# Channel attention, tile 0: where the rests, the row statistics and the second batch's projection stand

## The reference

```python
def _L0_xattn_ref(x, init, Wq, bq, Wk, bk, Wv, bv):   # init is ctx_4096
    q = jnp.einsum('dc,bct->btd', Wq, init) + bq
    k = jnp.einsum('dc,bct->bdt', Wk, init) + bk[None, :, None]
    R = jnp.einsum('btd,bds->bts', q, k)
    attention = jax.nn.softmax(R, axis=-1)
    v = jnp.einsum('oc,bct->bto', Wv, x) + bv
    return jnp.einsum('bts,bsc->bct', attention, v)
...
x = x + jnp.tanh(g_xattn[0]) * _L0_xattn_ref(_layernorm(x, axis=-1), ctx_4096, ...)
```

## Time and profile before

| what | value |
|---|---|
| median of 3 runs | 847.76 us (847.03 to 848.78) |
| the profiled execution's own time | 845.51 us |
| its span | 843.7 us |
| busy: PE, PEld | 774.3 us (92%), 613.4 us (73%) |
| busy: DVE, ACT, POOL | 662.9 us (79%), 352.3 us (42%), 380.9 us (45%) |
| HBM traffic | 44 GB/s over the span |

### The profile page before, as it was taken

One profiled execution on the slowest core, in us unless ns is written; L12 is line 12 of the kernel. 1 busy time (PEld: TensorE's weight loads), 2 busy tenths in 40 slices (PEclk: granted clock), 3 DMA queues, 4 the chain that ended last, 5 costly groups with the idle time before them and its releaser, 6 DMA issues.

```text
span 843.7 us, 12571 instructions
## 1 busy us (share of the span) xinstructions
PE 774.3 (92%) x4276; PEld 613.4 (73%) x4276; DVE 662.9 (79%) x1230; ACT 352.3 (42%) x1064; POOL 380.9 (45%) x324
## 2 busy tenths in 40 slices
PE   2898998888989999999999999999999999969975
PEld 1565565786867788888878888877888787757754
DVE  5788888888978877778788777787877778798972
ACT  2777776221334333333333333434333243237541
POOL 2787787415364433333253332434423333386541
PEclk9999999897999999999999999999999999989995
DMA  8310030101021111011020100102101020200101
GB/s 256 107 51 25 25 106 0 39 0 51 1 76 50 38 38 51 26 38 39 26 63 26 51 26 26 48 29 63 38 26 38 26 88 24 55 4 1 38 25 38
DMA packets 37460, 37.43 MB, mean 44 GB/s; under 512 B 2912, under 2 KB 27232, under 8 KB 37408
## 3 DMA queue, kind: packets, MB, share of 16 engines
q1 hardware_dynamic: 35184, 32.81, 13.3%
q10 hardware_dynamic: 2224, 3.94, 1.5%
HBM read 34.64 MB, written 2.10 MB: 44 GB/s over the span
## 4 chain that ended last, share of the span: by engine, by line
PE 63%; DVE 6%; POOL 4%; issue 3%; ACT 2%; POOLq 0%; DVEq 0%; ACTq 0%
PE QB L1478 6%; PE QB L1480 6%; PE SB L1598 6%; PE QB L1479 6%; PE ROW L1479 6%; PE ROW L1478 6%; PE ROW L1480 6%; PE KV L1478 4%; PE PB L1571 3%; PE KV L1479 3%; PE KV L1480 3%; DVE rope_b L1244 2%; PE KV L1662 2%; PE TB L1541 2%; POOL dense L976 1%
## 5 line engine op out<-in xcount | busy, mean ns | idle before, releaser
L976 POOL TENSOR_TENSOR dense<-rope_a,rope_b 128x512 f32<-128x512 f32 x62 | 79.4, 1280 | 167.5 <-DVE rope_b L1244 167.3
L1110 ACT ACTIVATE ot_hi<-PB 128x512 fp32r<-128x512 f32 x64 | 38.3, 599 | 198.4 <-PE PB L1571 198.2
L1101 ACT ACTIVATE e_sb<-masked,nmax 128x64 f32<-128x64 f32 x256 | 86.1, 337 | 58.1 <-DVE nmax L1273 57.7
L1478 PE MATMUL QB<-xT_hi,wq_lo 128*128 128x512 f32 x256 | 107.0, 418 | 0.0
L1479 PE MATMUL ROW<-wo_lo,ot_hi 128*128 128x512 f32 x256 | 101.7, 397 | 0.0
L1480 PE MATMUL QB<-xT_hi,wq_hi 128*128 128x512 f32 x256 | 101.7, 397 | 0.0
L1479 PE MATMUL QB<-xT_lo,wq_hi 128*128 128x512 f32 x256 | 101.5, 396 | 0.0
L1478 PE MATMUL ROW<-wo_hi,ot_lo 128*128 128x512 f32 x256 | 101.3, 396 | 0.0
L1480 PE MATMUL ROW<-wo_hi,ot_hi 128*128 128x512 f32 x256 | 101.0, 395 | 0.0
L1241 DVE TENSOR_TENSOR rope_a<-QB,rope 128x512 f32<-128x512 f32 x62 | 42.8, 691 | 72.7 <-PE QB L1480 72.5
L1282 DVE TENSOR_TENSOR p_sb<-e_sb,rz 128x256 f32<-128x256 f32 x64 | 86.8, 1356 | 2.2
(11 more groups left out here) (200 smaller groups left out, 1902.2 us busy)
## 6 DMA issues: line engine op xcount, KB each, us to landing
raw<-in_wq SPq DMA_DIRECT2D x32, 256.0 KB, 2.7
raw<-in_wo SPq DMA_DIRECT2D x32, 256.0 KB, 2.6
ctx_two<-in_ctx SPq DMA_DIRECT2D x16, 256.0 KB, 3.8
x_sb<-in_x SPq DMA_DIRECT2D x8, 256.0 KB, 7.1
ctx_raw<-in_ctxT ACTq DMA_DIRECT2D x1, 2048.0 KB, 12.9
raw<-in_wv SPq DMA_DIRECT2D x8, 256.0 KB, 2.7
raw<-in_wk SPq DMA_DIRECT2D x8, 256.0 KB, 2.9
out<-x_sb SPq DMA_DIRECT2D x8, 256.0 KB, 2.0
```

What stands on the lines that cost most here:

```text
L976: nc.gpsimd.tensor_tensor(dst, a, b, ALU.add).then_inc(s_rot, 1)
L1101: nc.scalar.activation(e_sb[:, r, :], masked[:, r, :], ACT.Exp, bias=nmax[:, r:r + 1], accum_out=zsum[:, r:r + 1]).then_inc(s_exp, 1)
L1478: nc.tensor.matmul(out, lhs[1], rhs[0], start=first, stop=False)
```

## The change

VectorE makes the two rests of tile 0's first batch ahead of any row statistics; of these it makes only those of tiles 0 and 1 in front of tile 0, and those of tiles 2 to 7 one by one in the units 2 to 7 of tile 0, behind the unit's maximum. The variance step and the power step are each made twice, for tiles 0 and 1 and for tiles 2 to 7; the second power step stands on GpSimd behind tile 0. Tile 0's second batch is projected behind the scores of unit 0 and rounded in unit 1. The eighth of ctx_raw that belongs to tile 0 is rounded in unit 7. GpSimd's tile 0 stands outside its loop. Three small loads are issued by SyncE behind the contexts.

```diff
@@ block.sync
                 load_ctx(t)
+            sp.dma_start(c["bias0"][:, :], d["bias0"].partition_broadcast(P)).then_inc(c["s_small"], 16)
+            sp.dma_start(c["assign_i"][:, :], d["assign"].partition_broadcast(CLUSTERS)).then_inc(c["s_small"], 16)
+            sp.dma_start(c["cluster_id"][:, :], d["cluster_ids"]).then_inc(c["s_small"], 16)
             load_ahead(sp, d, c)
@@ block.scalar, tile
-                    if u == PROJECT_B + 1:
+                    if u == (PROJECT_B + 1 if behind else 1):
                         qk_round(t, 2)
                         qk_round(t, 3)
...
-                    if u == OUTPUT:
+                    if u == (OUTPUT if behind else 7):
                         act.wait_ge(s_raw, 16)
                         nc.scalar.activation(ctx_hi[:, t, :], ctx_raw[:, t, :], ACT.Copy).then_inc(s_thi, 1)
@@ block.scalar
-            act.dma_start(c["bias0"][:, :], d["bias0"].partition_broadcast(P)).then_inc(c["s_small"], 16)
-            act.dma_start(c["assign_i"][:, :], d["assign"].partition_broadcast(CLUSTERS)).then_inc(c["s_small"], 16)
-            act.dma_start(c["cluster_id"][:, :], d["cluster_ids"]).then_inc(c["s_small"], 16)
@@ block.vector, tile
-                    if u == PROJECT_B + 1:
+                    if u == (PROJECT_B + 1 if behind else 1):
                         qk_rest(t, 2)
                         qk_rest(t, 3)
+                    if u >= 2 and not behind:
+                        dve.wait_ge(s_x[u], 16)
+                        row_sums(nc, dve, c, u, s_sum, s_mv, u)
                     if u == OUTPUT:
                         inverse(t, u)
-                        if not behind:
-                            dve.wait_ge(s_rstd, 1)
+                        if behind < 2:
+                            dve.wait_ge(s_rstd, behind + 1)
                         normalize(t)
...
+                if not behind:
+                    dve.wait_ge(s_mv, TILES)
+                    variance_eps(nc, c, s_var, 2, TILES)
@@ block.vector
-            for t in range(TILES):
+            qk_rest(0, 0)
+            qk_rest(0, 1)
+            for t in range(2):
                 dve.wait_ge(s_x[t], 16)
                 row_sums(nc, dve, c, t, s_sum, s_mv, t)
-            dve.wait_ge(s_mv, TILES)
-            variance_eps(nc, c, s_var)
-            qk_rest(0, 0)
-            qk_rest(0, 1)
+            dve.wait_ge(s_mv, 2)
+            variance_eps(nc, c, s_var, 0, 2)
@@ block.gpsimd
-            def tile(t, ahead):
+            def tile(t, ahead, first=False):
...
-                    if u == OUTPUT:
+                    if u == (7 if first else OUTPUT):
                         eighth_rest(t)
...
-            inverse_deviation(nc, pool, c, s_var, s_rstd)
-            with pool.Fori(0, TILES - 1) as t:
+            inverse_deviation(nc, pool, c, s_var, s_rstd, 0, 2)
+            tile(0, True, True)
+            inverse_deviation(nc, pool, c, s_var, s_rstd, 2, TILES, 2)
+            with pool.Fori(1, TILES - 1) as t:
                 tile(t, True)
@@ block.tensor, tile
-                    if u == PROJECT_B:
+                    if u == (PROJECT_B if behind else 0):
                         project(t, 2)
                         project(t, 3)
```

## The result

The kernel after takes 850.71 us (median of 14 runs, 848.36 to 853.05); the kernel before, run beside it, 846.00 us (14 runs, 844.37 to 848.78). The ratio estimated from these runs is 1.0045, with a 95% interval of 1.0034 to 1.0056, which is 3.8 us; the two medians themselves lie 4.71 us apart. Forecast were 3.4 us more, a ratio of 1.0040. The profiled execution took 850.24 us around a span of 848.2 us, 4.73 us above that of before.

The account below looks back on a forecast made before the run. VectorE, full from tile 0's sixth maximum to tile 1's first, was taken as the bound. Start -2.15 plus tile 0 longer +5.6 made +3.4 after rounding: 847.76 became 851.2 us; eight in ten, 848.9 to 853.4.

Parts of the forecast that it names:

- Start, -2.15: First score matmul: with the rests first, TensorE starts when w_v lands, at 15.65 instead of 17.80, a gain of 2.15 us.
- Early projection and moved stall: Tile 0, units 0 to 2: second maximum 19.5, VectorE's 1.4 us idle moved to unit 1, fourth maximum 2.2 us late.
- Path to the sixth maximum, 6.31 - 1.14: Tile 0, fourth to sixth maximum: 6.31 us loses two roundings of 1.14, so 5.17; sixth maximum at 29.7, 1.07 late.
- rival (5): TensorE's clock falls in the sparser tile 0; projections and scores take 1.2 us more, 852.4 us; chance 0.05.
- From the sixth maximum, +2.5: Sixth maximum to tile 1's first: three more pairs (2.4) and a variance step (0.1) lengthen VectorE's 4.88 us by 2.5.
- The cover of the pairs of units 3 and 4: VectorE's statistics there (1.6 us) lie under the path to the sixth maximum; without cover, nothing up to 1.6 more.
- GpSimd, taken as 0: Between tiles 0 and 1: eighth_rest and second power step, together 2.6 us, taken as 0, with 2.6 as bound.
- a sign of being wrong: The forecast is wrong if the shift at tile 1 is not the shift at the end of the stage.
- Variance step, taken as 0.1: End of tile 0: the new variance step shifts its follower by 0.1 us; bounds 0.1 and 1.1 beside a GpSimd product.
- Rival (2), statistics in the waits: The statistics vanish in VectorE's waits, tile 0 keeps its length, only the earlier start counts: 845.6 us; chance 0.06.
- Rival (6): Statistics stretched by GpSimd through the shared port, some 0.6 us for each of six, 3.9 us more: 855.1; chance 0.03.

Follow-up runs that it names:

- wv_early: The kernel after with the two transfers of w_v issued ahead of x; 846.37 us, ratio to before 0.9992.
- fill_more: The kernel after with 8, 8 and 16 unread matmuls added behind the scores of units 2, 3 and 4 of tile 0; 848.05 us, ratio to before 1.0018.
- eighth_back: The kernel after with tile 0's eighth of ctx_raw rounded in unit 3 and its rest made there by GpSimd, as before; 850.09 us, one execution.
- late_projection: The kernel after with the second batch projected behind unit 2 and its rests in unit 3, as before; 848.27 us, ratio to before 1.0022.
- no_six_pairs: The kernel after without the six statistics pairs of tiles 2 to 7, their mean and variance a constant 1; 848.72 us, ratio to before 1.0022.
- pair_per_tile_late_raw: The kernel before with w_v ahead of x, rests first, next tile's statistics made in each tile, ctx_raw and w_raw issued later; 843.60 us, ratio to before 0.9956.
- after_again: The kernel after, unchanged, timed again as a control; 849.68 us, ratio to before 1.0037.
- fill_idle_pe: The kernel after with six unread matmuls added behind the scores of each of units 2, 3 and 4 of tile 0; 849.00 us, ratio to before 1.0022.
- stats_ahead: The kernel after with all eight statistics pairs ahead of tile 0 again, but behind the two rests; 848.25 us, ratio to before 1.0012.

## Why the prediction was right, and where its sum was off

- *Start, -2.15.* Measured 2.09, with w_v as the releaser, and wv_early shows that it is w_v: issued sooner, it is no longer waited for. But w_v's landing varies: in the profiles of kernels that wait for it the first scores start between 14.74 (fill_more) and 16.36 (eighth_back).
- *Early projection and moved stall.* Second maximum forecast at 19.5, measured 19.53; q rest 21.6, measured 21.65; fourth maximum 24.55, measured 24.58, with the 1.35 us of waiting for ScalarE in its new place. This part of the sum held to 0.1 us.
- *Path to the sixth maximum, 6.31 - 1.14.* The step that failed. It was to be 5.17 and took 6.42. The roundings left it as forecast (ctx_two's at 25.95, 1.37 behind the fourth maximum, instead of 24.89 - 22.34 = 2.55), but the projection and the scores behind it ran at 1.2 GHz. This was rival (5), which I gave 0.05 and 1.2 us; in the profile it came true on top of the forecast, with 1.25 us, and 1.26 are gone in fill_more, where the clock stayed up. The Trainium skill, TensorE: Matmul & The Clock Gate, Why this matters for your kernels, warns of idle gaps between bursts. The traces agree in that the clock stayed up in fill_more, but the length of a single gap does not tell where it falls: a gap of 3.31 us came without a fall before and with one in late_projection, and in after the clock fell at 24.9 with no longer gap in tile 0 than the 1.12 us ahead of 23.24 (four transposes and two scores between 21.47 and 24.9). My evidence against the rival, one long gap at a high clock, was thus too little: one row of one execution does not rule the fall out.
- *From the sixth maximum, +2.5.* Measured 2.47. no_six_pairs gives 1.9 of it back (7.35 against 5.44 us); the other 0.5 of its three pairs went into its own slower variance step.
- *The cover of the pairs of units 3 and 4.* Without the pairs of units 2, 3 and 4 the sixth maximum comes 0.6 sooner, where 0.8 for that of unit 2 and nothing for the others was taken. This fits the forecast; no run has them apart. VectorE waited 2.30 us for the sixth scores in after and still 1.05 in fill_more, so the cover holds at the high clock too.
- *GpSimd, taken as 0.* It was 0.3, the very amount that the working named, shown by eighth_back. So the shift at tile 1 (4.82) is not quite that at the end of the stage (5.15), which the prediction had listed as a sign of being wrong. *Variance step, taken as 0.1:* right in after (its follower starts 0.07 behind it), but 0.56 in two experiments, within the bounds.
- *Rival (2), statistics in the waits.* Refuted by no_six_pairs, where tile 0 is 2.5 us shorter, and by tile 0's growth of 6.9 us. It is true of another place: in unit 3 of every tile they do fit (pair_per_tile_late_raw).
- *Rival (6).* Its 3.9 us come from the normalization's difference (1.19 - 0.53 = 0.66 us, six times), not from its ratio, as the prediction says; by the ratio, 0.68 us would become 1.5, and the end some 5 us later. It did not happen: the statistics took 0.66 to 0.70 us.
- *The size.* In the profiles tile 1's first maximum is 4.82 us late and the stage's end 5.15, not 3.4: the clock's 1.25 and GpSimd's 0.3 were missing. The profiled executions keep 4.73 of it, the medians 4.71, the ratio 3.8, and after_again gives 2.75 by its medians and 3.1 by its ratio. That 3.4 lies among these is in part luck. So is the nearness of 851.2 to 850.71: the forecast stood on a median of 847.76 from three runs of the kernel before, of which fourteen had 846.00. The part behind the stage varies in one kernel by as much as is looked for: from the last update to the end of the span it is 693.3 and 691.9 us in the two profiles of before, and 692.6 and 691.7 in those of after. And both profiles of before are of quick executions, while in six of the seven other timings of kernels built on after the shift at the stage's end exceeds the difference of the medians by 2 to 4 us (in no_six_pairs by 1.1). Whether slower executions of before lose some of this in tile 0 is open.

## What to carry to other kernels

Work moved off the front of a pipeline into its steady part is free only in a slot where that engine waits, after everything that it would delay; find the slot in the waits, unit by unit, before placing the work (here unit 3's 1.36 us took a bn_stats in each tile; in units 5 to 7 of tile 0 each pair cost nearly its full time). When the first wait of a start-up goes, look at once for the next one: two 16 KB loads behind 2 MB held back 3.8 of 6 us. When a stage gets sparser for TensorE, price its matmuls at both clock levels. When two profiles are compared, look where each execution lies among its kernel's times.

## What the runs showed of the hardware

- Matmuls that nobody reads can shorten a stretch: in fill_more, with 32 of 256 columns put into TensorE's waits, the granted clock stayed at 2.4 GHz up to 36.2 us, and from the first scores to tile 1's first maximum it took 21.38 us instead of 22.64. In fill_idle_pe, with 18, the clock fell at 28.0 and it took 22.64.
- The same wait of TensorE, 3.31 us for the k rest, came without a fall of the clock in both profiles of before and with one in late_projection (from 23.9 to 30.7).
- A variance step of 128x6, a plain tensor-scalar operation, took 0.16 us in after, where GpSimd was idle, and 0.64 in stats_ahead and no_six_pairs, where GpSimd was in the midst of a product of 1.04; bn_stats stayed at 0.66 to 0.70 in all profiles. The normalization took 1.18 before, all of it beside GpSimd's context rest, and 0.55 at 26.17 in after, where GpSimd was idle from 26.43. The Trainium skill, Advanced Engine Details and Errata, Mode Summary, has two-port modes of VectorE and GpSimd block each other; for these two operations the traces agree, and that bn_stats is not held up is a measurement of these runs alone.
- Where TensorE's start waits for w_v, its landing alone moved that start by 1.6 us between profiles (14.74 to 16.36), while whole executions of the kernel after spread over 4.7 us (848.36 to 853.05).
